# Attention kernel with two branches and a mixture of experts: scores for the maxima of two heads in one pair of wide matmuls

## The chip, the cores and the metric

The kernel runs on one core of one Trainium2 chip. The metric is the device time of one launch in microseconds, the median of several runs. Shares and stretches of the trace are of one profiled execution, whose own time stands beside the median below.

## What is computed

The input is 8 batches of 256 tokens of width 256. Each batch is normalised and goes through two attention branches of 16 heads, a latent one with rotary parts ("MLA") and a plain one with heads of 16 numbers ("MHA"); behind the plain one comes a mixture of 8 experts, top 2 per token. In the reference, cut to what matters here:

```python
xn = _layernorm(x)
s = _L0_attn_ref(xn, ...)                      # MLA, 16 heads, causal softmax
# plain branch (MHA), then the experts
q = (xn1 @ Wq.T).reshape(b, s, 16, 16); k, v likewise
attn = jnp.einsum('bqhd,bkhd->bhqk', q, k) * scale
attn = softmax(where(causal, attn, -inf))
h = jnp.einsum('bhqk,bkhd->bqhd', attn, v).reshape(b, s, hid)
x2 = residual + h @ Wo.T
out = x + s * silu(x2 + moe(rmsnorm(x2)))
```

The change touches the scores of the plain branch alone.

## The kernel before, in words

Every engine runs its own instruction list in program order, and semaphores tie the lists together. A batch b goes through four stages on TensorE (PE):

- **P2(b)**, `stage_p2`: the queries and keys of the plain branch, stacked 64 rows high per head (high part, low part, a row for the maximum), are transposed. There are 8 units u = 0 to 7, four transposes of 128x128 each, queries for even u and keys for odd u, into PSUM banks 3, 2, 0 in turn (`bank2`). ScalarE (ACT) copies each unit out, and VectorE (DVE) copies the lower 64 partitions of the units that hold queries (`odd_heads`). Between u = 0 and u = 1 PE also runs `to_tokens` of the batch before; DVE then makes `normalise` of it, behind its third `odd_heads`, and PE's `back` of it, first thing after the first head of T1, waits for that.
- **T1(b)**, `stage_t1`: for each of the 16 heads h, PE makes the transposed scores of the MLA branch (`scores1`, four FP32 matmul instructions), then `max2(b)` for head h - 1: the untransposed scores of the plain branch, from which DVE takes each query's maximum (`maxima`, a 128-column and a 256-column reduction per head). ACT exponentiates, GpSimd (POOL) masks, and `values(g)` multiplies by the values after heads 7, 11, 15 and after the stage. Other work is hung between heads by number: on PE `back` (0), `project` (3), `transpose_x` (10), `route_transpose` (11), `route_logits` (14); on DVE, in `stage_m2`, the residual `kept` (4), `stats_x2` (5), `copy_batch` (7), `copy_rms1` (8), `scale_x2` (9), `x_low` (12), and `top_two` behind the stage.
- **P1(b + 1)**, `stage_p1`: projections of the next batch in 18 steps. `values(3)` and the transposes of the maxima (`max_t`) come after step 0; step 1 waits for `ohd`, the end of DVE's `top_two`.
- **T2(b)**, `stage_t2`: transposed scores of the plain branch (`scores2`) with the maxima of the next batch's MLA branch between them (`max1`). It starts when the row of maxima, sent by `row2` through the DMA queue, has landed.

The last batch has no P1. After it come the experts.

In `max2`, head h uses bank 2 + h % 2 of PSUM (`ps[2]`, `ps[3]`), and its matmuls wait until DVE has done head h - 2 (`mx2`). A matmul here is 128 stationary columns (queries) against 128 or 256 moving columns (keys). The two heads of a pair lie in the upper and the lower 64 partitions: `kt2` holds both, `qt2` holds each head by itself with zeros in the other half, cleared once at the start.

Of the kernel before, what the change touches and what calls it, by code (L numbers as in the profile page):

```python
# [23 lines left out]
F32 = mybir.dt.float32  # L24
# [7 lines left out]
P = 128  # L32
# [58 lines left out]
def build(nc, x, w_cols, w_dq, w_uqr, w_dkv, w_ukv, w_out, w_o, w_ln1, w_ln2, w_r, w_experts,  # L91
          cosines, sines, ident, mask, upper, route_c, slots, out):
    ctx = ExitStack()
    with ctx:
# [80 lines left out]
        wo2 = sb("wo2", [P, ET, E], F32, late)  # L175
        qt2 = sb("qt2", [P, H, S], F32R, late)
        kt2 = sb("kt2", [P, H // 2, S], F32R, late)
        v2 = sb("v2", [P, 2, H, PADV], F32, late)
# [97 lines left out]
        t2e = sem("mha_qk_kept")  # L276
        t2o = sem("mha_q_odd_kept")
        m2d = sem("mha_scores")
# [83 lines left out]
        def _(sp):  # L362
# [21 lines left out]
            def row2(b):  # L384
                sp.wait_ge(mte2, b + 1)
                for e in range(2):
                    r = ST * e + MROW2
                    sp.dma_start(qt2[r:r + 1, e:H:2, :].bitcast(F32),
                                 mt[e * H // 2:(e + 1) * H // 2, :]).then_inc(md2, 16)
# [78 lines left out]
        def _(pool):  # L468
# [14 lines left out]
            nc.gpsimd.memset(ks[:, :, :, MROW2:MROW2 + 1].bitcast(F32), 1.0)  # L483
            nc.gpsimd.memset(qt2[:, :, :].bitcast(F32), 0.0).then_inc(clear, 1)

# [98 lines left out]
        def _(pe):  # L584
# [115 lines left out]
            def stage_p2(b, after):  # L700

                max_t(b, negm1, mx1, mtr1)
                for u in range(8):
# [4 lines left out]
                    if u >= 3:  # L708

                        wait(pe, t2e, 8 * b + u - 2)  # L710
                        if (u - 3) % 2 == 0:
                            wait(pe, t2o, 4 * b + (u - 3) // 2 + 1)
# [25 lines left out]
            def max2(b):  # L738
                def head(h):
                    if h == 0:  # L740
                        wait(pe, t2e, 8 * b + 8)
                        wait(pe, t2o, 4 * b + 4)
                    if h >= 2:
                        wait(pe, mx2, 16 * b + h - 1)
                    raw_scores(ps[2 + h % 2], qt2[:, h, :], kt2[:, h // 2, :]).then_inc(m2d, 1)
                return head
# [37 lines left out]
            def scores2(h, o):  # L784
                mm(o[:, 0:2 * P], kt2[:, h // 2, P:S], qt2[:, h, :], True, True)
                return mm(o[:, 2 * P:4 * P], kt2[:, h // 2, 0:P], qt2[:, h, :], True, True)

# [181 lines left out]
        def _(act):  # L969
# [100 lines left out]
            def stage_p2(b, after):  # L1070
                max_t1(b)
                wait(act, st2, 16 * b)
                for u in range(8):
                    wait(act, tr2, 8 * b + u + 1)
                    t = slice(u // 4 * P, (u // 4 + 1) * P)
                    a = bank2(u)[:, :].rearrange("p (h t) -> p h t", h=4)
                    if u % 2 == 0:

                        h0 = 8 * (u // 2 % 2)
                        copy(qt2[0:ST, h0:h0 + 8:2, t], a[0:ST, :, :]).then_inc(t2e, 1)  # L1080
                    else:
                        copy(kt2[:, 4 * (u // 2 % 2):4 * (u // 2 % 2) + 4, t], a).then_inc(t2e, 1)
                    after.get(u, lambda: None)()
# [151 lines left out]
        def _(dve):  # L1235
# [152 lines left out]
            def stage_m2(b, after):  # L1388
                wait(dve, mtr2, b)
                for h in range(H):  # L1390
                    maxima(b, h, (h % 2) * (H // 2) + h // 2, negm2, m2d, mx2)
                    after.get(h, lambda: None)()

# [26 lines left out]
            def odd_heads(b, i):  # L1420

                wait(dve, tr2, 8 * b + 2 * i + 1)
                t = slice(i // 2 * P, (i // 2 + 1) * P)
                h0 = 8 * (i % 2)
                copy(qt2[ST:P, h0 + 1:h0 + 8:2, t],
                     bank2(2 * i)[ST:P, :].rearrange("p (h t) -> p h t", h=4)).then_inc(t2o, 1)

# [320 lines left out]
```

## Time and profile before

| | us |
|---|---|
| median of 3 runs | 956.92 |
| lowest, highest | 955.44, 962.53 |
| profiled execution | 958.59 |
| its span, first to last instruction | 956.9 |
| mean granted TensorE clock | 0.935 of full |

The page gives busy time by engine, the span in slices, the DMA queues, the chain of work that ended last, and groups of instructions by line. `L586` is the helper that issues every matmul, so matmuls are told apart by their tiles and widths. Buffer numbers are left out of the names: `qt` stands for `qt` and `qt2`, `kt` for `kt` and `kt2`. "ps<-kt,qt" are the products of `max2` (keys moving), "ps<-qt,kt" those of `scores1` and `scores2`.

### The profile page before, as it was taken

The numbers are of one execution on the slowest core, as the hardware profiler recorded it, in microseconds if no ns is written. First come the engines' busy times: TensorE is split into PE (matmuls) and PEld (weight loads), VectorE is DVE, ScalarE is ACT, GpSimd is POOL, SyncE is SP. The second block draws the span as 40 slices with busy tenths as digits, with TensorE's granted clock in tenths as the row PEclk, the third lists the DMA queues.
The fourth block names the chain that finished last, engine by engine and source line by source line (L and its number), as shares of the span: only waits on it lengthen the run. The fifth ranks groups of instructions, "written<-read, shape, count | busy, mean of one in ns | idle before, by whom it ended". The sixth has DMA issues, their size and how long they took to land.

```text
span 956.9 us, 18123 instructions
## 1 busy us (share of the span) xinstructions
PE 830.5 (87%) x6432; PEld 743.6 (78%) x6432; DVE 625.2 (65%) x2207; ACT 501.6 (52%) x1089; POOL 392.2 (41%) x538
## 2 busy tenths in 40 slices
PE   5889999999999999999998998965269999998980
PEld 3868978978887887887897897843169999998980
DVE  4876677667677667757758757632257777776754
ACT  3445375366366456456356446540146677776651
POOL 5522432343343334344344344331404756555541
PEclk9878999999999999999999999976579999999995
DMA  8000000000000000000000000030236776889736
GB/s 273 1 1 2 13 1 25 12 2 13 24 1 14 13 13 2 24 12 3 23 13 2 24 12 3 23 144 23 47 134 176 221 220 198 238 240 348 193 53 186
DMA packets 39884, 71.04 MB, mean 74 GB/s; under 512 B 10914, under 2 KB 34850, under 8 KB 36834
## 3 DMA queue, kind: packets, MB, share of 16 engines
q1 hardware_dynamic: 29074, 57.39, 17.6%
q0 software_dynamic: 9856, 12.13, 6.7%
q8 instruction: 52, 0.85, 0.4%
q10 hardware_dynamic: 864, 0.36, 0.2%
q14 instruction: 38, 0.31, 0.1%
HBM read 55.12 MB, written 14.81 MB: 73 GB/s over the span
## 4 chain that ended last, share of the span: by engine, by line
PE 67%; DVE 10%; DMA 9%; issue 6%; POOL 2%; ACT 2%; SPq 2%; POOLq 0%; DVEq 0%; ACTq 0%
PE ps L586 54%; DMA expert_rows<-yo,slot_of 6%; PE ps L679 6%; PE ps L716 3%; DVE ps L1400 2%; PE ps L612 2%; DVE ps L1397 1%; SPq L425 1%; PE ps L621 1%; DVE qr L1237 1%; DMA w_ukv_raw<-in_w_ukv 1%; DMA raw<-in_w_experts 1%; SPq L441 1%; POOL slots L515 1%; POOL expert_rows L563 1%
## 5 line engine op out<-in xcount | busy, mean ns | idle before, releaser
L523 POOL TENSOR_SCALAR_AFFINE_SELECT ex<-ex 128x256 f32<-128x256 f32 x256 | 107.6, 425 | 246.5 <-ACT ex L1101 245.1
L1101 ACT ACTIVATE ex<-ps 128x384 f32<-128x384 f32 x256 | 125.4, 497 | 118.9 <-PE ps L586 116.8
L586 PE MATMUL ps<-qt,kt 128*128 128x256 f32 (+1 forms) x768 | 164.1, 325 | 8.6 <-ACT ex L1101 4.6
L502 POOL TENSOR_TENSOR tok<-tok,swp 128x256 f32<-128x256 f32 x128 | 97.4, 761 | 114.7 <-DVE swp L1362 113.7
L1397 DVE CUSTOM_DVE_ANT_0 ps<-ps,mask 128x128 f32<-128x128 f32 x256 | 77.4, 302 | 94.9 <-PE ps L586 90.5
L586 PEld LDWEIGHTS ps<-qt,kt 128*128 128x128 f32 x768 | 108.9, 193 | 20.7 <-issue 9.8
L563 POOL DMA_INDIRECT expert_rows<-yo,slot_of x46 | 78.5, 1707 | 110.8 <-DMA expert_rows<-yo,slot_of 55.6
L1400 DVE CUSTOM_DVE_ANT_0 ps<-ps,mask 128x256 f32<-128x256 f32 x256 | 118.9, 465 | 0.0
L1241 DVE TENSOR_TENSOR wel<-raw,weh 128x768 fp32r<-128x768 f32 x92 | 88.4, 961 | 37.2 <-ACT weh L971 36.0
L586 PE MATMUL ps<-wh,xth 128*128 128x320 f32 (+2 forms) x352 | 96.9, 358 | 3.7 <-DVE wl L1241 2.8
L1358 DVE TENSOR_TENSOR tok<-ps,cos_t 128x320 f32<-128x320 f32 x128 | 62.9, 491 | 52.8 <-PE ps L586 52.2
L586 PE MATMUL ps<-xeh,weh 128*128 128x256 f32 x368 | 79.4, 298 | 11.8 <-issue 9.9
L971 ACT ACTIVATE qt<-ps 128x512 f32<-128x512 f32 (+1 forms) x96 | 57.2, 596 | 61.9 <-PE ps L679 59.8
L971 ACT ACTIVATE kt<-ps 128x512 f32<-128x512 f32 (+1 forms) x96 | 57.4, 598 | 53.4 <-PE ps L679 48.3
L586 PE MATMUL ps<-wh,xtl 128*128 128x320 f32 (+2 forms) x352 | 84.1, 321 | 0.0
L586 PE MATMUL ps<-wl,xth 128*128 128x320 f32 (+2 forms) x352 | 83.8, 320 | 0.0
L971 ACT ACTIVATE weh<-raw 128x768 fp32r<-128x768 f32 x92 | 77.9, 846 | 10.1 <-DMA raw<-in_w_experts 10.1
L679 PE MATMUL ps<-idf,tok 128*128 128x128 f32 x512 | 77.0, 273 | 0.0
L586 PE MATMUL ps<-xeh,wel 128*128 128x256 f32 x368 | 75.9, 289 | 0.0
L586 PE MATMUL ps<-xel,weh 128*128 128x256 f32 x368 | 75.8, 288 | 0.0
L586 PE MATMUL ps<-kt,qt 128*128 128x128 f32 (+1 forms) x256 | 73.4, 368 | 0.0
L586 PE MATMUL ps<-kr,qr 128*128 128x128 f32 (+1 forms) x256 | 58.6, 316 | 16.8 <-DVE negm L1400 13.1
(160 smaller groups left out, 1918.3 us busy)
## 6 DMA issues: line engine op xcount, KB each, us to landing
raw<-in_w_experts SPq DMA_DIRECT2D x23, 1536.0 KB
mla_branch<-s_b SPq DMA_DIRECT2D x8, 256.0 KB, 2.1
expert_rows<-xn SPq DMA_DIRECT2D x8, 256.0 KB, 2.2
x_normalised<-otk SPq DMA_DIRECT2D x8, 256.0 KB, 2.1
xr<-in_x SPq DMA_DIRECT2D x1, 2048.0 KB
s_tok<-mla_branch SPq DMA_DIRECT2D x1, 2048.0 KB
w_cols_raw<-in_w_cols SPq DMA_DIRECT2D x1, 1792.0 KB, 15.4
x<-expert_rows SPq DMA_DIRECT2D x3, 512.0 KB, 5.2
```

The source lines that it names most:

```text
L502: nc.gpsimd.tensor_tensor(t, t, swp[:, n % 2, :, :], ALU.add).then_inc(tokd, 1)
L523: nc.gpsimd.affine_select(a, a, [[0, 2], [1, P]], ALU.is_ge, zero, 0, -1).then_inc(exm, 1)
L563: nc.gpsimd.indirect_dma_start(ys[:, :], bass.IndirectOffsetOnAxis(mt_b[:, blk, j, 1:2], 0), yo[:, blk % 2, j, :], None, compute_op=ALU.ad ...
L586: return nc.tensor.matmul(o, a, m, start=start, stop=stop, skip_group_check=True, **k)
L679: t = nc.tensor.transpose(ps[2 + n % 2][:, j * P:(j + 1) * P], tok[:, n % 4, j, :], idf[:, :])
L716: i = nc.tensor.transpose(bank2(u)[:, j * P:(j + 1) * P], a[:, p0:p0 + P], idf[:, :])
L971: return nc.scalar.activation(o, a, ACT.Copy)
L1101: nc.scalar.activation(ex[:, h % (2 * G), :], ps[4 + h % 2][:, P:4 * P], ACT.Exp, scale=scale).then_inc(ex_, 1)
L1241: return nc.vector.tensor_tensor(o, a, b.bitcast(F32), ALU.subtract)
L1358: nc.vector.tensor_tensor(tok[:, n % 4, :, 0:HW], a, cos_t[:, tt:tt + 1, :].broadcast_to([P, G, HW]), ALU.mult)
L1397: nc.vector.tensor_tensor_reduce(out=o[:, 0:P], in0=o[:, 0:P], in1=mask2[:, 1, :], scale=-1.0, scalar=-2.0 * BIG, op0=ALU.add, op1=ALU.min ...
L1400: nc.vector.tensor_tensor_reduce(out=o[:, S:2 * S], in0=o[:, S:2 * S], in1=mask2[:, :, :].rearrange("p a k -> p (a k)"), scale=-1.0, scala ...
```

## The change

The plain branch's queries are now kept in pairs (`qt2` has 8 columns of heads, both heads of a pair in it) and the keys per head with zeros in the other half (`kt2` has 16). One matmul with a pair's queries stationary and both heads' keys moving gives the scores of both heads: 256 columns for the first 128 queries (into `ps[3]`), 512 for the other 128 (into `ps[2]`). `max2` does nothing after even heads and issues both matmuls of a pair after the odd one; the first waits for DVE to have done the 128-wide reductions of the pair before, the second for its 256-wide ones. DVE reduces in the order first queries of both heads, other queries of both heads; its hung work keeps its numbers, counted now in half pairs. `odd_heads` now copies halves of the key units (odd u), so that each waits one unit longer. `scores2` reads pairs and heads the other way round, with the same sizes.

```diff
             def row2(b):
                 for e in range(2):
                     r = ST * e + MROW2
-                    sp.dma_start(qt2[r:r + 1, e:H:2, :].bitcast(F32),
+                    sp.dma_start(qt2[r:r + 1, :, :].bitcast(F32),
...
                         wait(pe, t2e, 8 * b + u - 2)
-                        if (u - 3) % 2 == 0:
+                        if (u - 3) % 2 == 1:
                             wait(pe, t2o, 4 * b + (u - 3) // 2 + 1)
...
             def max2(b):
                 def head(h):
-                    if h == 0:
+                    if h % 2 == 0:
+                        return
+                    j = h // 2
+                    if j == 0:
                         wait(pe, t2e, 8 * b + 8)
                         wait(pe, t2o, 4 * b + 4)
-                    if h >= 2:
-                        wait(pe, mx2, 16 * b + h - 1)
-                    raw_scores(ps[2 + h % 2], qt2[:, h, :], kt2[:, h // 2, :]).then_inc(m2d, 1)
+                    else:
+                        wait(pe, mx2, 16 * b + 2 * j - 1)
+                    mm(ps[3][:, 0:2 * P].rearrange("p (e k) -> p e k", e=2), qt2[:, j, 0:P],
+                       kt2[:, 2 * j:2 * j + 2, 0:P], True, True).then_inc(m2d, 1)
+                    if j > 0:
+                        wait(pe, mx2, 16 * b + 2 * j)
+                    mm(ps[2][:, :].rearrange("p (e k) -> p e k", e=2), qt2[:, j, P:S],
+                       kt2[:, 2 * j:2 * j + 2, :], True, True).then_inc(m2d, 1)
...
             def scores2(h, o):
-                mm(o[:, 0:2 * P], kt2[:, h // 2, P:S], qt2[:, h, :], True, True)
-                return mm(o[:, 2 * P:4 * P], kt2[:, h // 2, 0:P], qt2[:, h, :], True, True)
+                mm(o[:, 0:2 * P], kt2[:, h, P:S], qt2[:, h // 2, :], True, True)
+                return mm(o[:, 2 * P:4 * P], kt2[:, h, 0:P], qt2[:, h // 2, :], True, True)
...
                     if u % 2 == 0:
+                        copy(qt2[:, 4 * (u // 2 % 2):4 * (u // 2 % 2) + 4, t], a).then_inc(t2e, 1)
+                    else:
                         h0 = 8 * (u // 2 % 2)
-                        copy(qt2[0:ST, h0:h0 + 8:2, t], a[0:ST, :, :]).then_inc(t2e, 1)
-                    else:
-                        copy(kt2[:, 4 * (u // 2 % 2):4 * (u // 2 % 2) + 4, t], a).then_inc(t2e, 1)
+                        copy(kt2[0:ST, h0:h0 + 8:2, t], a[0:ST, :, :]).then_inc(t2e, 1)
...
             def stage_m2(b, after):
                 wait(dve, mtr2, b)
-                for h in range(H):
-                    maxima(b, h, (h % 2) * (H // 2) + h // 2, negm2, m2d, mx2)
-                    after.get(h, lambda: None)()
+                for j in range(H // 2):
+                    for t in range(2):
+                        wait(dve, m2d, 16 * b + 2 * j + t + 1)
+                        n = (t + 1) * P
+                        for e in range(2):
+                            o = ps[3 - t][:, e * n:(e + 1) * n]
+                            col = e * (H // 2) + j
+                            i = nc.vector.tensor_tensor_reduce(
+                                out=o, in0=o, in1=mask2[:, 1 - t:2, :].rearrange("p a k -> p (a k)"), scale=-1.0,
+                                scalar=-2.0 * BIG, op0=ALU.add, op1=ALU.min, accum_out=negm2[:, t, col:col + 1])
+                        i.then_inc(mx2, 1)
+                        after.get(2 * j + t, lambda: None)()
...
             def odd_heads(b, i):
-                wait(dve, tr2, 8 * b + 2 * i + 1)
+                wait(dve, tr2, 8 * b + 2 * i + 2)
                 t = slice(i // 2 * P, (i // 2 + 1) * P)
                 h0 = 8 * (i % 2)
-                copy(qt2[ST:P, h0 + 1:h0 + 8:2, t],
-                     bank2(2 * i)[ST:P, :].rearrange("p (h t) -> p h t", h=4)).then_inc(t2o, 1)
+                copy(kt2[ST:P, h0 + 1:h0 + 8:2, t],
+                     bank2(2 * i + 1)[ST:P, :].rearrange("p (h t) -> p h t", h=4)).then_inc(t2o, 1)
```

The clearing at the start moves from `qt2` to `kt2`, which now has the larger of the two sizes.

## Rows read from the trace of the kernel before

**Rows 1.** The page: busy us (share of the span) and instructions of each engine.

```profile
PE 830.5 (87%) x6432; PEld 743.6 (78%) x6432; DVE 625.2 (65%) x2207; ACT 501.6 (52%) x1089; POOL 392.2 (41%) x538
```

**Rows 2.** Busy time by stretch: us, busy us (instructions) per engine, clock, DMA share, GB/s.

```profile
219.86:294.39 74.53, 71.31 (x584) 62.54 (x582) 51.82 (x224) 40.16 (x87) 30.05 (x53) 1.00 0.04 13
294.39:370.44 76.05, 72.85 (x584) 64.05 (x583) 51.83 (x224) 40.16 (x87) 30.06 (x53) 0.98 0.04 12
...
298.99:322.82 23.83, 23.46 (x198) 19.69 (x196) 16.99 (x90) 12.04 (x28) 7.25 (x17) 1.00 0.07 24
```

**Rows 3.** Timeline, PE in T1(3): start us, us, instruction, count [idle before, releaser].

```profile
305.37 0.82 PE L586 MATMUL ps<-qt,kt 128*128 128x128 f32 x4
306.03 0.19 PEld L586 LDWEIGHTS ps<-kt,qt 128*128 128x128 f32 x1
306.14 0.31 PEld L586 LDWEIGHTS ps<-qt,kt 128*128 128x128 f32 x2
306.26 0.27 PE L586 MATMUL ps<-qt,kt 128*128 128x128 f32 x1
```

**Rows 4.** Timeline, PE in P1: matmuls of 512 moving columns.

```profile
347.65 0.63 PE L586 MATMUL ps<-wl,xth 128*128 128x512 f32 x2
348.12 0.63 PE L586 MATMUL ps<-wh,xtl 128*128 128x512 f32 x2
```

**Rows 5.** Timeline, DVE in T1(3): head 4, `kept`, head 6, `copy_batch`.

```profile
306.46 0.30 DVE L1397 CUSTOM_DVE_ANT_0 ps<-ps,mask 128x128 f32<-128x128 f32 x1
...
306.68 0.47 DVE L1400 CUSTOM_DVE_ANT_0 ps<-ps,mask 128x256 f32<-128x256 f32 x1
...
307.06 0.69 DVE L1342 TENSOR_TENSOR xn<-ps,xn 128x512 f32<-128x512 f32 x1
...
309.58 0.29 DVE L1397 CUSTOM_DVE_ANT_0 ps<-ps,mask 128x128 f32<-128x128 f32 x1
...
310.81 0.71 DVE L1237 COPY xb<-xn 128x512 f32<-128x512 f32 x1
```

**Rows 6.** Timeline, PE and DVE at the end of P2(3): units 4 and 5, `odd_heads`, `normalise`, `back`.

```profile
297.01 0.64 PE L716 MATMUL ps<-idf,qs 128*128 128x128 f32 x4
297.61 0.63 PE L716 MATMUL ps<-idf,ks 128*128 128x128 f32 x4
297.68 0.69 DVE L1237 CAST qt<-ps 64x512 fp32r<-64x512 f32 x1 [0.21 <-PE ps L716]
...
298.41 0.37 DVE L1322 RECIPROCAL rec<-ps 128x16 f32<-128x16 f32 x2
...
298.81 0.76 DVE L1327 TENSOR_TENSOR otk<-ps,rec 128x256 f32<-128x256 f32 x2
...
299.62 0.42 PEld L621 LDWEIGHTS ps<-idf,otk 128*128 128x128 f32 x4 [0.21 <-DVE otk L1327]
```

**Rows 7.** Timeline, PE and DVE, second half of T1(3) and start of P1(4).

```profile
311.66 0.30 PE L645 MATMUL ps<-idf,xb 128*128 128x128 f32 x1
...
317.44 1.06 PE L586 MATMUL ps<-wr,s_b 128*128 128x8 f32 x8 [0.23 <-ACT s_b L971]
...
320.20 0.50 PE L586 MATMUL ps<-kt,qt 128*128 128x128 f32 x2
...
320.74 0.30 DVE L1397 CUSTOM_DVE_ANT_0 ps<-ps,mask 128x128 f32<-128x128 f32 x1 [0.47 <-PE ps L586]
...
321.33 0.17 DVE L1502 MAX8 mx<-ps 128x8 f32<-128x8 f32 x1
...
322.60 0.17 DVE L1516 TENSOR_TENSOR ohb<-oh 128x16 bf16<-128x16 f32 x1
...
322.82 0.56 PE L586 MATMUL ps<-wh,xth 128*128 128x320 f32 x2
```

**Rows 8.** PE after a wait in T2: timeline, then busy time by stretch (columns of group 2).

```profile
354.26 0.77 PE L586 MATMUL ps<-kr,qr 128*128 128x128 f32 x2 [1.11 <-DVE negm L1400]
...
354.15:357.56 3.41, 3.30 (x15) 3.33 (x16) 2.35 (x15) 0.00 (x0) 0.29 (x1) 0.50 0.03 5
```

More of the change, by code:

```diff
@@ L175, in build @@
         wo2 = sb("wo2", [P, ET, E], F32, late)
-        qt2 = sb("qt2", [P, H, S], F32R, late)
-        kt2 = sb("kt2", [P, H // 2, S], F32R, late)
+        qt2 = sb("qt2", [P, H // 2, S], F32R, late)
+        kt2 = sb("kt2", [P, H, S], F32R, late)
         v2 = sb("v2", [P, 2, H, PADV], F32, late)
@@ L276, in build @@
         t2e = sem("mha_qk_kept")
-        t2o = sem("mha_q_odd_kept")
+        t2o = sem("mha_k_odd_kept")
         m2d = sem("mha_scores")
@@ L483, in _ @@
             nc.gpsimd.memset(ks[:, :, :, MROW2:MROW2 + 1].bitcast(F32), 1.0)
-            nc.gpsimd.memset(qt2[:, :, :].bitcast(F32), 0.0).then_inc(clear, 1)
+            nc.gpsimd.memset(kt2[:, :, :].bitcast(F32), 0.0).then_inc(clear, 1)
             def power(k, t):
```

## The prediction

> **What bounds the kernel now.** I read the page first: PE is the busiest engine, 87% of the span [rows 1]. Then busy time by stretch: a middle batch takes 74.5 us, or 76.0 when the granted clock falls to half once inside it [rows 2]; six of the eight batches have this shape. In T1, the stage that the change is about, PE is busy 23.46 of 23.83 us [rows 2]: it is the bound, and DVE, busy 16.99, is the next to be looked at. Last I read the timeline of T1 of the third batch (starting at 294.39), on which all times below stand. The reader should see three things in it: what a head costs PE, how early DVE delivers what PE waits for, and the three places where PE already meets DVE or ACT.
>
> **What PE saves.** One head of `max2` costs PE 0.23 us: its second load of queries starts at 306.03, the next load at 306.14, and the next head's scores at 306.26 [rows 3]. So the 128-column product holds the array for 0.11, as long as the next load takes, and the 256-column one for 0.12. Two heads cost 0.46. After the change a pair has one product of 256 columns, 0.12, and one of 512, whose price is read where the same type (FP32R) is used at that width: two of them take 348.12 - 347.65 = 0.47, so 0.235 each [rows 4]. The loads hide under the products before them (0.11 under 0.12, under 0.235 and under the last product of `scores1`). Pair: 0.35. Gain: 0.11 per pair, 8 pairs, 8 batches: 64 x 0.11 = 6.9 us if nothing else moves. The keys of a pair are read as two runs of 128 or one of 512 columns; no row shows what two runs cost. Bounds: nothing below, and above the rate of the FP32 products of `scores1`, 0.66 us for 768 columns [rows 3], or 0.66 for the pair, which would lose 0.2 per pair, 13 us. I take 0.35, since type and length are those of the nearest row.
>
> The Trainium skill (TensorE: Matmul & The Clock Gate, Back-to-back issue gap) gives about 131 ns per product of 512 columns in a stream of loads and products. By that figure, as an estimate, the second product would cost 0.10 less and the gain would be some 6.6 us larger; the trace's own 0.235 does not agree, and the sum goes by the trace.
>
> **What it costs at the front of T1.** The third `odd_heads` now waits for unit 5 instead of unit 4. Unit 4 starts at 297.01, unit 5 at 297.61, and DVE starts the copy 0.67 after unit 4 began [rows 6]. So the copy moves by 0.60. Right behind it on DVE are the reciprocals (298.41) and the products of `normalise` (298.81 + 0.76), and PE's `back` is already waiting for them, 0.21 idle [rows 6]. Nothing covers this: `back` goes from 299.62 to 300.22, and all of T1 behind it with it. +0.60 in the seven batches that have `normalise`. Unit 4 now waits for DVE's copy of half of unit 1, 0.69 long [rows 6], beside ACT's: a tenth at most, left out. The fourth `odd_heads` has over a microsecond before the first pair needs it. What ACT copies in P2 has the same sizes in another order, and `scores2`, the clearing and `row2` keep their sizes: nothing.
>
> **What it costs in the middle.** DVE's work per head is 0.60 (306.46 to 307.06) [rows 5], 1.20 per pair. Before, a head's matmuls waited for the head two before them, 1.78 earlier, which DVE had done after 1.06, so 0.7 was to spare; now the second product of a pair waits for the whole pair before. DVE starts 306.46 - 306.14 = 0.32 after the 256-column product gets the array [rows 3, 5], and is done 0.32 + 1.20 + 0.14 = 1.66 after it. The next pair comes 2 x 0.66 + 0.35 = 1.66 later, its second product at 1.78. It just fits, with nothing to spare for DVE's hung work. From head 4 on this work is dense. Heads 4 to 7 with `kept` and `stats_x2` run without a break from 306.46 to 310.81, 4.35 us [rows 5], and then comes `copy_batch`, 0.71, for which `transpose_x` waits.
>
> After the change DVE can start heads 4 and 5 only when pair 2 is there. Before, the product of head 5 reached the array at 306.26 + 0.66 = 306.92. Now: + 0.60 (front) - 0.22 (two pairs saved) - 0.23 (head 4 is no longer ahead of it) = 307.07. DVE starts at 307.39 and reaches `copy_batch` 4.35 later, at 311.74. The same point is the end of pair 3, so pair 4's second product cannot start before about 311.74 + 0.14 + 0.1 = 311.98. `transpose_x`, right behind it, stood at 311.66 [rows 7] and would be due at 311.66 + 0.60 - 5 x 0.11 = 311.71, so the product was due 0.235 earlier, at 311.48: a stall of 0.5. `transpose_x` then waits for the copy until 311.74 + 0.71 = 312.45 and starts near 312.53 instead of 311.66. So the whole loss at this point is +0.87, and it already contains the 0.60 of the front and the gain of five pairs. `values(0)` also waits for `kept`, some 0.4, which the same stall absorbs. Pair 5 gives back 0.11: +0.76.
>
> **What it costs at the end.** The routing products, which wait for ACT, not PE (0.23 idle at 317.44 [rows 7]), shift by that 0.76; what PE gains just before them is lost in their wait. Head 14's product, 0.23, is gone from behind them. The last pair therefore comes at 320.20 + 0.76 - 0.23 = 320.73. Before, DVE began the last head 0.54 after its first load and worked 0.59, to 321.33 [rows 7]. Now it begins 0.11 + 0.32 = 0.43 after the load, and has two heads, 1.20: 322.36. `top_two` is 322.60 + 0.17 - 321.33 = 1.44 long, and step 1 of P1 starts 0.05 after it, at 322.82 [rows 7]. After: 322.36 + 1.44 + 0.05 = 323.85. **+1.0 us per middle batch.** From there PE's order and loads are as before.
>
> **The sum.** Batches 1 to 6 (counted from 0): 6 x 1.03 = +6.2. Batch 0 has no `normalise`, no hung work of the routing and no `top_two`: the whole gain, -0.9. The last batch has no `copy_batch`: front +0.60, six pairs -0.65, the stall +0.5, head 14 -0.23, the longer tail of DVE (1.63 instead of 1.13) +0.5: +0.6 to +0.7. Together +5.9 us on the profiled execution's 958.59 (956.9 span and 1.7 around it), or +0.6%. That execution is 1.7 above the median; on the median, 956.92 + 5.9 = 962.8 us.
>
> **The clock.** After 1.11 us of idle at 354.26 the granted clock is 0.50 for 3.41 us, the lower of its two levels, 1.2 GHz [rows 8]; a batch with such a drop takes 76.05 instead of 74.53, 1.5 us more [rows 2]. Three of the six middle batches have one; others have a wait as long without it. The new stalls, 0.8 at `back`, 0.4 and 0.5 around pair 4, 0.7 before step 1, are shorter, so I take no new drops; but shifts decide which waits cost one, and 1.5 us more or less per batch is open.
>
> **Rivals.**
> - *PE's saving alone counts.* DVE's lateness is hidden: `normalise` was not the last thing that `back` needed, and the hung work fits in between. Then -6.9 us: 950.0. For it: PE is 98% busy in T1. Against: `back` waits for DVE already [rows 6]. It decides if unit 5 ends no later than DVE could use it. Faster, but within 1%. 0.10.
> - *Only one of the two costs is real.* Without the front's 0.60 the middle stall grows as DVE is then the bound from pair 2 on, but all shifts by 0.60 less: +5.9 - 7 x 0.6 = +1.7, 958.6. Without the longer tail of DVE (0.5 each): +5.9 - 3.5 = +2.4, 959.3. Together 0.20.
> - *The stalls pull the clock down.* The stall at pair 4 and the wait for the copy lie within 1.2 us of each other. If they cost one drop in each of the seven batches: +5.9 + 7 x 1.5 = +16.4, 973.3; in three or four of them, 968. For it: 0.8 us idle there against 1.11 where a drop was seen. Against: products lie between. 0.18.
> - *The wide product is slow* on keys in two runs, up to 0.66 for a pair: past the point where a pair costs 0.46 PE loses in every batch, up to +13 more. 0.03.
> - *The wide product is quick*, less than half of [rows 4]: some 6.6 more gained than in the first rival, 943. Nothing in the trace speaks for it: 0.01. That is what the page of the Trainium skill named above would give.
> - My forecast, 962.8, its own range 960 to 966: 0.48.
>
> **Chances and range.** Within 1% is about what a measurement of this kernel can tell from no change: 947.3 to 966.5. Slower by over 1% are most of the clock rival, the slow product, and the upper edge of mine with a drop or two: 0.22. Faster by over 1% needs the quick product or the first rival with fewer drops: 0.03. The rest, 0.75, lies within. The range reaches from near the first rival to the middle of the clock rival: 952 to 970.
>
> **What would show it.** In the trace of the changed kernel: products of `max2` 0.12 and 0.235 apart; `back` waiting 0.8 for DVE where it waited 0.21; a wait of PE for `negm` before the fifth pair and for `xb` before `transpose_x`; step 1 of P1 about 29.4 us after the batch's first transpose instead of 28.4; batches of 75.5 us, or 77 with a clock drop. It is wrong if `back` keeps its place, if T1 shows no wait for `negm`, or if batches are shorter than 74.5.

## The result and the profile after

| | kernel before | kernel after |
|---|---|---|
| median | 956.18 us | 968.49 us |
| lowest to highest of 4 runs each | 954.51 to 962.53 | 966.96 to 974.06 |
| profiled execution | 958.59 us | 969.09 us |
| its span | 956.9 us | 967.4 us |
| middle batch without, with a clock drop | 74.5, 76.0 us | 76.0, 77.5 us |

The ratio is 1.0127, with a 95% interval of 1.0065 to 1.0189: slower by 1.3%. The same kernel measured again beside the experiments gave 968.32 us and a ratio of 1.0092 [1.0056, 1.0129]. So the loss is certain and its size is about 1%. The forecast was 962.8, with a range of 952 to 970: the sign was right, the size about half of what came. (The medians differ by 12.3 us here and by 8.8 in the repetition, the profiled spans by 10.5; the accounts below go by the spans.) One of the 32 runs of the kernel before beside the later experiments (1195 us) and one of the 12 of `e6_all` (1355 us) were slow, at a granted clock of 0.64 and 0.55; the ratios leave them out.

The page of the kernel after, busy us and instructions of each engine:

```profile
PE 827.1 (85%) x6304; PEld 727.4 (75%) x6304; DVE 624.8 (65%) x2207; ACT 501.5 (52%) x1089; POOL 391.2 (40%) x538
```

Against [rows 1] PE has 128 matmuls fewer and is busy 3.4 us less, while the span is 10.5 us longer. DVE and ACT have the same work as before. So what was lost is waiting, not work, and it has to be looked for in idle time. Busy time by stretch (us, busy us and instructions of PE, PE's loads, DVE, ACT, POOL; clock, DMA share, GB/s), batches 2 and 3:

```profile
220.92:298.47 77.55, 72.68 (x567) 62.09 (x566) 52.07 (x224) 40.28 (x87) 29.81 (x53) 0.98 0.04 12
298.47:374.49 76.02, 71.08 (x568) 60.79 (x567) 51.96 (x224) 40.18 (x87) 29.79 (x53) 1.00 0.04 12
```

Beside [rows 2], batches without a drop: 76.02 us instead of 74.53, with PE busy 71.08 instead of 71.31. PE's idle time went from 3.2 to 4.9 us per batch. What PE waited for in batches 1 to 6 (releaser: us in total, times, longest us):

```profile
PE ps L586 <- DVE negm L1417: 10.5, 12, 1.5
PE ps L586 <- DVE ohb L1533: 3.2, 6, 0.6
...
PE ps L621 <- DVE otk L1335: 2.5, 6, 0.4
PE ps L586 <- DVE xn L1350: 2.3, 6, 0.4
```

Once in each batch: 0.53 for the rows that `top_two` writes (`ohb`) ahead of step 1, 0.41 at `back` (`otk`), 0.39 at `values(0)` for `kept` (`xn`). The first line is a wait in T2, in another part of the batch; the same line of the kernel before is

```profile
PE ps L586 <- DVE negm L1400: 8.9, 12, 1.5
```

It grew by 1.6 us, and the forecast had nothing there.

**T1 of the same batch as in [rows 3] to [rows 7].** It starts at 298.47 here and at 294.39 there, so a time of before has its place 4.08 later. PE:

```profile
304.37 0.66 PE L621 MATMUL ps<-idf,otk 128*128 128x128 f32 x4 [0.41 <-DVE otk L1335]
...
312.83 0.86 PE L586 MATMUL ps<-ex,v 128*32 128x256 f32 x16 [0.39 <-DVE xn L1350]
...
315.85 0.78 PE L586 MATMUL ps<-kt,qt 128*128 128x256 f32 x2
316.73 0.63 PE L645 MATMUL ps<-idf,xb 128*128 128x128 f32 x4
...
322.40 1.06 PE L586 MATMUL ps<-wr,s_b 128*128 128x8 f32 x8 [0.28 <-ACT s_b L979]
...
328.07 0.56 PE L586 MATMUL ps<-wh,xth 128*128 128x320 f32 x2 [0.53 <-DVE ohb L1533]
```

DVE:

```profile
303.15 0.37 DVE L1330 RECIPROCAL rec<-ps 128x16 f32<-128x16 f32 x2
...
315.93 0.66 DVE L1245 COPY xb<-xn 128x512 f32<-128x512 f32 x1
...
325.36 0.30 DVE L1405 CUSTOM_DVE_ANT_0 ps<-ps,mask 128x128 f32<-128x128 f32 x1 [1.56 <-PE ps L586]
...
326.59 0.17 DVE L1519 MAX8 mx<-ps 128x8 f32<-128x8 f32 x1
...
327.84 0.17 DVE L1533 TENSOR_TENSOR ohb<-oh 128x16 bf16<-128x16 f32 x1
```

Measured from the batch's start, the points that the forecast named, in us (the profiled executions; the same in all six middle batches to a few hundredths):

| point | before | after | shift | forecast |
|---|---|---|---|---|
| `back` [rows 6] | 5.25 | 5.90 | +0.65 | +0.60 |
| `transpose_x` [rows 7] | 17.27 | 18.26 | +0.99 | +0.87 |
| routing products [rows 7] | 23.05 | 23.93 | +0.88 | +0.76 |
| step 1 of P1 [rows 7] | 28.43 | 29.60 | +1.17 | +1.03 |

The transposes of the maxima, which follow the last pair and on which the experiments are also read, went from 27.90 to 28.68. The chain of the forecast is there link by link. The reciprocals begin 0.66 later and `back` idles 0.41. `copy_batch` (315.93) ends at 316.59, and `transpose_x`, which stands behind it, starts at 316.73. The last pair's reductions run from 325.36 to the MAX8 of `top_two` at 326.59, 1.23 for two heads where [rows 7] has 0.59 for one, and step 1 starts 0.06 after `ohb` is done.

Two of the signs that the forecast named have to be looked at closely. `back` idles 0.41 on PE; the 0.8 of the forecast is the wait of its loads, 0.81 here, which stood at 0.21 before. And T1 shows no wait of PE for `negm`, which the forecast had called a sign that it is wrong. All that is left of this wait is small: the load of the second product of a pair that follows right on another waits 0.10 (at 311.29, for DVE's end of the pair before), and costs PE 0.06.

### The profile page after: what moved, and what is told of

Read it like the earlier page. It is cut to its first block, busy times and chain, and to the rows that moved or that the text cites. A ratio compares the mean times of both kernels' runs of the same rounds, so it can differ in the third digit from the quotient of the medians.

```text
span 967.4 us, 17859 instructions
## 1 busy us (share of the span) xinstructions
PE 827.1 (85%) x6304; PEld 727.4 (75%) x6304; DVE 624.8 (65%) x2207; ACT 501.5 (52%) x1089; POOL 391.2 (40%) x538
## 4 chain that ended last, share of the span: by engine, by line
PE 53%; DMA 14%; DVE 14%; issue 11%; POOL 4%; ACT 2%; SPq 1%; POOLq 0%; DVEq 0%; ACTq 0%
PE ps L586 41%; DMA expert_rows<-yo,slot_of 11%; PE ps L679 5%; PE ps L716 3%; DVE ps L1417 2%; PE ps L612 2%; POOL expert_rows L563 1%; DVE ps L1405 1%; DVE ps L1414 1%; DMA ln<-in_w_ln 1%; POOL xg L552 1%; PE ps L621 1%; DVE qr L1245 1%; POOL slots L515 1%; DVE otk L1335 1%
## 5 line engine op out<-in xcount | busy, mean ns | idle before, releaser
L586 PE MATMUL ps<-qt,kt 128*128 128x256 f32 (+1 forms) x768 | 160.6, 328 | 8.4 <-ACT ex L1109 4.4
L586 PEld LDWEIGHTS ps<-qt,kt 128*128 128x128 f32 x768 | 115.0, 195 | 24.8 <-ACT ex L1109 9.9
L1405 DVE CUSTOM_DVE_ANT_0 ps<-ps,mask 128x128 f32<-128x128 f32 (+1 forms) x256 | 85.0, 385 | 57.1 <-PE ps L586 56.9
L1196 ACT ACTIVATE sg<-ps 128x256 f32<-128x256 f32 x92 | 35.7, 388 | 70.5 <-PE ps L586 67.8
L586 PEld LDWEIGHTS ps<-xeh,weh 128*128 128x128 f32 x368 | 58.2, 196 | 15.8 <-issue 15.8
```

The lines of the kernel that those rows point to most:

```text
L586: return nc.tensor.matmul(o, a, m, start=start, stop=stop, skip_group_check=True, **k)
L1196: nc.scalar.activation(sg[:, n % 2, :], ps[n % 3][:, 0:BS], ACT.Silu).then_inc(sgd, 1)
L1405: i = nc.vector.tensor_tensor_reduce(out=o, in0=o, in1=mask2[:, 1 - t:2, :].rearrange("p a k -> p (a k)"), scale=-1.0, scalar=-2.0 * BIG, ...
```

## The experiments

Nine kernels were made of the two, each run beside the kernel before; the kernel after was run once more with them. What is read from each is the place of a point after its batch's start, in the profile, and the median of its runs.

| kernel | `back` | `transpose_x` | maxima transposes | step 1 | PE's wait in T2 | batch, no drop | ratio to before |
|---|---|---|---|---|---|---|---|
| before | 5.25 | 17.27 | 27.90 | 28.43 | 1.11 or 1.48 | 74.5 | 1 |
| after | 5.90 | 18.26 | 28.68 | 29.60 | 1.48 | 76.02 | 1.0127 |
| `e8_after_again` | 5.90 | 18.27 | 28.68 | 29.61 | 1.48 | 76.03 | 1.0092 |
| `e1_layout` | 5.90 | 17.94 | 28.56 | 29.09 | 1.48 | 75.55 | 1.0055 |
| `e2_norm_first` | 5.32 | 17.63 | 28.05 | 28.98 | 1.48 | 75.41 | 1.0031 |
| `e3_top_early` | 5.90 | 18.27 | 28.68 | 28.82 | 1.11 or 1.49 | 74.88 | 1.0061 |
| `e4_base_late` | 5.90 | 18.27 | 28.68 | 29.61 | 1.10 | 75.66 | 1.0058 |
| `e5_copy_early` | 5.90 | 18.00 | 28.47 | 29.40 | 1.49, once 1.11 | 75.87 | 1.0081 |
| `e6_all` | 5.32 | 17.37 | 27.84 | 27.98 | 1.11 | 74.05 | 0.9963 |
| `e7_before_moves` | 5.25 | 17.28 | 27.87 | 28.02 | 1.10 | 74.04 | 0.9942 |
| `e9_pairs_clean` | 5.32 | 16.91 | 26.85 | 27.00 | 1.10 | 73.02 | 0.9899 |
| `e10_heads_clean` | 5.25 | 17.27 | 27.37 | 27.51 | 1.10 | 73.73 | 0.9965 |

The 73.73 of `e10_heads_clean` is of batch 1, its only one without a drop. Batch 1 is about 0.2 longer than the later ones in other kernels too (76.22 and 76.03 in `e8_after_again`), so its later batches would be near 73.5.

### The new layout with products per head (`e1_layout`)

Queries stay in pairs and keys padded, `odd_heads` and its waits are those of after; only the products go by head, and DVE reduces head by head as in the kernel before.

```diff
-                    mm(ps[3][:, 0:2 * P]..., qt2[:, j, 0:P], kt2[:, 2 * j:2 * j + 2, 0:P], True, True)
...
-                    mm(ps[2][:, :]..., qt2[:, j, P:S], kt2[:, 2 * j:2 * j + 2, :], True, True)
+                    raw_scores(ps[2 + h % 2], qt2[:, h // 2, :], kt2[:, h, :]).then_inc(m2d, 1)
```

> The new layout (queries in pairs, keys padded) and the later odd_heads, but max2 and stage_m2 head by head as before: 128 and 256 columns per head. Theory (the later copy delays normalise and back by 0.6, and the rest of the loss is the pairing): back 5.9 us after the batch's first transpose (before 5.25, after 5.90), step 1 of P1 at 28.4 + 0.6 = 29.0 (before 28.4, after 29.6), median 956.2 + 7 x 0.6 = 960.5; if the wait for DVE in T2 stays at 1.48 instead of 1.12, 2 more. Rival (the front costs nothing in the end, the pairs alone do): step 1 at 28.4, 956 to 957. Other rival (the padded keys themselves are slower in scores2 or max2): over 966 with longer products.

Measured: `back` +0.65, step 1 at 29.09, 964.31 us (10 runs; before beside it 959.29), ratio 1.0055 [1.0033, 1.0077]. Of e1's timeline, `back` and step 1 of P1, the batch from 297.24:

```profile
303.14 0.44 PE L621 MATMUL ps<-idf,otk 128*128 128x128 f32 x2 [0.42 <-DVE otk L1327]
...
326.33 0.56 PE L586 MATMUL ps<-wh,xth 128*128 128x320 f32 x2
```

The shift is the same at `back` (0.65) and at step 1 (29.09 - 28.43 = 0.66): the layout alone costs the front and nothing behind it. From here to the kernel after, the wide products make step 1 another 0.51 later, where their saving on PE should have made it earlier. The loss in T1 thus has two parts of about equal size, one of the layout, one of the wide products.

### `normalise` ahead of the third copy of the odd heads (`e2_norm_first`)

```diff
                 odd_heads(b, 1)
+                normalise()
                 odd_heads(b, 2)
-                normalise()
                 odd_heads(b, 3)
```

> The changed kernel with normalise ahead of the third odd_heads on DVE. Theory: back no longer waits for DVE, 5.05 instead of 5.90 after the first transpose, and since DVE's dense stretch is tied to pair 2, which comes earlier with it, step 1 of P1 moves by the same 0.85 to 28.75; seven batches: 968.5 - 6 = 962.5. Rival (T1 is bound by DVE or ACT further on, which start no earlier): back early but step 1 still at 29.3 or later, 966 to 968.5.

Measured: `back` at 5.32, step 1 at 28.98, 962.72 us (10 runs), ratio 1.0031 [1.0003, 1.006]. `back` and step 1 in e2's timeline, the batch from 293.92:

```profile
299.24 0.60 PE L621 MATMUL ps<-idf,otk 128*128 128x128 f32 x4
...
322.90 0.56 PE L586 MATMUL ps<-wh,xth 128*128 128x320 f32 x2 [0.53 <-DVE ohb L1533]
```

The wait at `back` is gone and T1 ends 0.62 earlier, all of what `back` gained (0.58), and no more: the front was a pure shift, and the end's wait of 0.53 is untouched by it. `back` did not come to the expected 5.05: it now stands right behind the first head's scores, as in the kernel before, and these start 0.06 later than there (4.66 after the batch's start instead of 4.60). That is what the layout costs in P2 apart from `normalise`: unit 4 starts at 2.86 instead of 2.62, and most of it is caught up by unit 7.

### `top_two` ahead of the last pair (`e3_top_early`)

```diff
+                if not first:
+                    after[13] = lambda: top_two(b - 1)
                 stage_m2(b, after)
-                if not first:
-                    top_two(b - 1)
```

> The changed kernel with top_two moved ahead of the last pair's reductions, into DVE's idle 1.6 us. Theory (step 1 waits for DVE's longer tail, two heads instead of one, plus top_two): step 1 comes right behind the transposes of the maxima, 28.95 instead of 29.6; six batches: 968.5 - 4 = 964.5. Rival (the tail is not what step 1 waits for, or the reductions of the last pair are pushed back by top_two and the transposes with them): 29.4 to 29.6, 967 to 969.

Measured: maxima transposes unchanged at 28.68, step 1 at 28.82, 964.36 us (10 runs), ratio 1.0061 [1.0038, 1.0084]. e3's timeline, the batch from 293.09:

```profile
321.77 0.39 PE L602 MATMUL ps<-idf,negm 128*16 128x128 f32 x2
321.91 0.54 PE L586 MATMUL ps<-wh,xth 128*128 128x320 f32 x2
```

Step 1 follows the transposes by 0.14 with no wait, where it was 0.92 in the kernel after. So 0.78 of T1's end was `top_two` standing behind the tail of DVE. In the kernel before the same distance was 0.53: part of this wait was there all along.

### The update of `base` behind the casts (`e4_base_late`)

This is the step in T2 that the forecast did not have. In `positions`, DVE adds the counts to `base` ahead of the casts to `meta`; here it does so after them, and the counts that DVE and PE wait for are moved with it.

```diff
                 dve.wait_ge(pst, 6 * r + 2)
-                nc.vector.tensor_tensor(base[:, :], ps[1][:, 2 * NE:3 * NE], base[:, :], ALU.add)...
...
                 i.then_inc(pst, 1)
+                nc.vector.tensor_tensor(base[:, :], ps[1][:, 2 * NE:3 * NE], base[:, :], ALU.add)...
```

> The changed kernel with the update of base in positions moved behind the two casts to meta, so that these casts reach DVE 0.08 to 0.2 us earlier against POOL's select. Theory (in T2 the second cast is held up for 0.24 us when POOL's select has started 34 to 41 ns after the first cast, and not when it starts 44 to 46 ns after it): the wait of PE in T2 falls from 1.48 to 1.1 in all six middle batches, 968.5 - 2.2 = 966.3, and fewer clock drops. Rival (the longer wait in T2 comes of something else that the change moved, POOL only happens to be there): the wait stays at 1.48 or moves by 0.1, 968 to 969.

Measured: T1 unchanged (29.61), PE's wait in T2 1.10 in all six middle batches, a batch 75.66 instead of 76.02, 964.92 us (10 runs), ratio 1.0058 [1.0034, 1.0082]. The result is the expected one, but the casts came earlier by far less than the 0.08 to 0.2 expected: 2.393 to 2.396 us after the product of the ranks instead of 2.400 to 2.407, some 0.01. That this was enough is described in the last section.

### `copy_batch` by the second head (`e5_copy_early`)

```diff
-                    after[7] = lambda: copy_batch(b + 1)
+                    after[1] = lambda: copy_batch(b + 1)
```

> The changed kernel with copy_batch hung behind the first pair (number 1) instead of number 7, where DVE is idle for 1.8 us. Theory (transpose_x waits for the copy, and DVE's dense stretch before it holds up the fifth pair): transpose_x goes from 18.26 after the batch's first transpose to 17.9, step 1 from 29.6 to 29.25; six batches: 2 us less than the changed kernel. The 0.4 that values(0) waits for kept stays. Rival (ScalarE's routing copy is what the rest of T1 waits for, so the gain is lost there): step 1 at 29.5 or later, no change.

Measured: `transpose_x` at 18.00, step 1 at 29.40, 965.67 us (10 runs; before 959.49), ratio 1.0081 [1.0054, 1.0107]. In e5's timeline, the batch from 299.57, the wait for `kept` is still there:

```profile
313.94 0.86 PE L586 MATMUL ps<-ex,v 128*32 128x256 f32 x16 [0.38 <-DVE xn L1350]
...
317.57 0.60 PE L645 MATMUL ps<-idf,xb 128*128 128x128 f32 x4
```

Taking the copy away from `transpose_x` gains 0.26 there and 0.20 at step 1, less than the 0.35 expected. Of the waits, the one for `kept` is left in the middle; `e9_pairs_clean` below moves it, together with `stats_x2`.

### All four moves on the pairs (`e6_all`) and on the kernel before (`e7_before_moves`)

`e6_all` is the kernel after with the edits of e2, e3, e4 and e5. `e7_before_moves` is the kernel before with those of e3, e4 and e5 (in its order `normalise` has no later copy ahead of it).

> The changed kernel with all four moves: normalise first, top_two early, base late, copy_batch early. Theory (each wait is its own, and they add): step 1 at 29.6 - 0.6 - 0.8 - 0.35 = 27.9, wait in T2 at 1.1, a middle batch without a clock drop 74.0 instead of 76.0, and 0.5 shorter than the kernel before: 0.995 of it. Rival (the moves hide behind each other, since one bound lies beneath all of them): step 1 at 28.3 to 28.8 and no faster than the kernel before.

> The kernel before with the moves that it allows: top_two early, base late, copy_batch early (normalise has to stay behind the third odd_heads there, as the bank of unit 4 is needed for unit 7). Tells whether the pairs are worth anything once the waits are gone. Theory: step 1 28.43 - 0.3 = 28.1, wait in T2 at 1.1 in all batches, middle batch 74.2: 0.997 of the kernel before, 0.2 us per batch more than with pairs. Rival (the pairs save their 0.11 each once nothing waits): e6_all ahead by 0.9 us per batch, 0.6%.

Measured: `e6_all` 955.57 us (12 runs), ratio 0.9963 [0.9941, 0.9984]; `e7_before_moves` 954.04 (12 runs), ratio 0.9942 [0.9918, 0.9967]; both beside 959.49 of before. Busy time by stretch of an undropped batch, e6:

```profile
215.80:289.85 74.05, 70.52 (x567) 60.97 (x566) 51.55 (x224) 40.08 (x87) 30.10 (x53) 1.00 0.04 13
```

and e7:

```profile
217.51:291.55 74.04, 71.02 (x583) 62.49 (x582) 52.01 (x224) 40.11 (x87) 29.92 (x53) 1.00 0.04 13
```

Three things follow. The waits of T1 add: step 1 gains 0.62 (e2) + 0.78 (e3) + 0.20 (e5) = 1.60 one by one, and 29.60 - 27.98 = 1.62 together. With these waits out of the way the pairs are a little faster than the kernel before. But the kernel before gains the same from the same moves: 74.04 and 74.05 for a batch, where PE is busy 0.5 less with the pairs. The pairs' saving is still lost in a wait. e6's timeline, the batch from 289.85, shows two:

```profile
303.59 0.86 PE L586 MATMUL ps<-ex,v 128*32 128x256 f32 x16 [0.37 <-DVE xn L1350]
...
312.94 1.06 PE L586 MATMUL ps<-wr,s_b 128*128 128x8 f32 x8 [0.27 <-ACT s_b L979]
```

### The waits for `kept` and for ACT out of the way (`e9_pairs_clean`, `e10_heads_clean`)

On `e6_all`, DVE's `kept` moves behind the first pair, `stats_x2` behind the second, and on ACT `keep_yt` one head earlier. `e10_heads_clean` is `e7_before_moves` with `keep_yt` moved alone; it has no wait for `kept`.

```diff
-                    after[13] = lambda: keep_yt(b - 1)
+                    after[12] = lambda: keep_yt(b - 1)
...
-                    after[1] = lambda: copy_batch(b + 1)
+                    after[1] = lambda: (copy_batch(b + 1), kept())
```

> e6_all with the last three waits of PE in T1 taken away: kept and copy_batch behind the first pair, stats_x2 behind the second, ScalarE's routing copy keep_yt one head earlier. In e6_all PE still waited 0.37 us for kept before values(0), 0.3 for scale_x2 and 0.4 for keep_yt. Theory (the pairs do save about 0.1 each, and each of these waits gave it back): transposes of the maxima at 27.1 to 27.3 after the batch's first transpose instead of 27.84, middle batch 73.5 instead of 74.05, 0.992 to 0.993 of the kernel before. Rival (in T1 ScalarE's exponentials and DVE's reductions of the pair before set the pace, so the pairs cannot save): 27.6 or later, 0.995 or more.

> e7_before_moves, head by head, with keep_yt one head earlier as well: the same moves on the kernel before. Theory: transposes of the maxima at 27.5 instead of 27.87, middle batch 73.7, 0.992 to 0.993 of the kernel before; e9_pairs_clean then 0.2 to 0.3 us per batch ahead, 0.1 to 0.2% of the whole. Rival (the pairs cannot save): e10_heads_clean as fast or ahead.

Measured: `e9_pairs_clean` 950.07 us (6 runs; before 958.99), ratio 0.9899 [0.9873, 0.9925]; `e10_heads_clean` 955.28 us (11 runs), ratio 0.9965 [0.9949, 0.998]. e9, the batch from 292.48, routing products without a wait and the maxima transposes:

```profile
314.68 0.95 PE L586 MATMUL ps<-wr,s_b 128*128 128x8 f32 x8
...
319.31 0.39 PE L602 MATMUL ps<-idf,negm 128*16 128x128 f32 x2
```

e10, the batch from 216.76, the same transposes:

```profile
244.13 0.39 PE L602 MATMUL ps<-idf,negm 128*16 128x128 f32 x2
```

The maxima transposes stand at 26.85 and 27.37, and the pairs are further ahead than the 0.2 to 0.3 expected. With no wait of PE shown in T1 of either, the eight pairs save 0.52 us per batch, 0.065 each. (The two kernels also differ in the layout, 0.07 at `back` against the pairs, and in the place of `normalise`, `kept` and `stats_x2`.) `e9_pairs_clean` is the fastest kernel of the study, 1.0% below the kernel before and 1.9% below the kernel after (950.07 against 968.32, both near a median of before of 959). Not all of the 5.2 us between e9's and e10's medians need be the pairs: of the 5.5 between their profiled spans, 6 x 0.52 = 3.1 are the pairs', and 3 are clock drops, of which e9 has three in the middle batches and e10 five, at 1.5 us each (the last batch and the experts took 0.6 more in e9).

### The kernel after once more (`e8_after_again`)

> The changed kernel as it is, beside the others on one chip, for its ratio from more runs. By the stretches of its trace, without clock drops and with the long wait in T2 in all six middle batches against two of six: 6 x 1.16 + 4 x 0.37 + 0.7 = 9.1 us, 1.009 to 1.010. If the drops also come more often with the longer wait, 1.012 or more.

Measured: 968.32 us (9 runs, before 959.49 in 32), ratio 1.0092 [1.0056, 1.0129]; every point of T1 within 0.01 of the first profile, T2's wait 1.48 in all six batches, three clock drops. The shares of T1 and T2 below are thus no accident of one execution. Those of the start and the end of the span are: here batch 0 ends at 141.49 and not at 143.19, and the last batch and the experts take 362.92 and not 361.78.

## Why the prediction was right, and where it was not

The two spans differ by 967.4 - 956.9 = 10.5 us. They split like this, against +5.9 forecast:

| part | forecast | measured | how |
|---|---|---|---|
| up to the end of batch 0 | -0.9 | -0.06 | 63.58 instead of 63.64 from the first scores on, which start at 79.61 in both |
| T1, batches 1 to 6 | +6.2 | +7.0 | 6 x 1.17 |
| T2's wait, batches 1 to 6 | 0 | +1.5 | 1.48 instead of 1.11 in four batches |
| clock drops, batches 1 to 6 | 0 | +1.5 | four instead of three |
| last batch and experts | +0.6 | +0.7 | 361.78 instead of 361.07 |
| sum | +5.9 | +10.6 | |

Two rows of this table owe something to luck. That the first scores start at 79.61 in both is chance (77.91 in `e8_after_again`). And the last row agrees by chance: at the end of T1 of the last batch the loss is twice the forecast, +1.39 (transposes of the maxima 28.06 after the batch's start instead of 26.67; 28.07 in `e8_after_again`), and what comes after it happened to be shorter. From that batch's start to the end of the program the twelve profiles lie between 357.86 and 365.12, and one kernel's two at 361.78 and 362.92. The forecast of this batch lacked two new waits of PE, 0.41 for `scale_x2` and 0.45 for the last maxima.

**The front** was right: forecast +0.60, measured +0.65, and e2, which moves `normalise` ahead of the later copy alone, gives back 0.58. The other 0.07 is the wait of unit 4, which the forecast had seen and left out. The rival that only one of the two costs is real falls with e2 and e3 together: each gives back its own share, 0.62 and 0.78.

**The middle** was right in size, +0.87 against +0.99, and in its cause, DVE's work between the pairs and `transpose_x`: DVE's stretch from the start of pair 2 (311.54) to `copy_batch` (315.93) took 4.39 where 4.35 was forecast. The order of PE's waits was another. The forecast put a stall of 0.5 before the second product of pair 4, with the wait for `kept` inside it. In the trace the wait for `kept` comes first (0.39 at 312.83), pair 4 then looks as in batch 0, where neither `kept` nor `stats_x2` hangs ahead of it (its two products take 0.78, and 0.77 there), and the rest is the wait for the copy, from the end of pair 4 to 316.73. e5 confirms the copy as the smaller part (0.20 of step 1). e9 against e6 moves `kept` and `stats_x2` (and `keep_yt`): `transpose_x` comes 0.46 earlier, 16.91 instead of 17.37, and `keep_yt` has no part in that (17.28 and 17.27 in e7 and e10).

**The end** was right in its mechanism, and e3 shows its whole price, 0.78. The forecast had +1.03 at this point and +1.17 was measured; 0.05 of the difference is the front; 0.07 more is already there at `transpose_x`; the last 0.02 is not traced.

**PE's saving** is the term that was mis-sized: 0.11 for every pair, 6.9 us in all. The price of a pair that waits for nothing was right. Two pairs with scores between them, in T1 of the batch from 298.47:

```profile
309.37 0.70 PE L586 MATMUL ps<-kt,qt 128*128 128x256 f32 x2
309.91 1.47 PE L586 MATMUL ps<-qt,kt 128*128 128x128 f32 x8
311.03 0.76 PE L586 MATMUL ps<-kt,qt 128*128 128x256 f32 x2
311.63 0.82 PE L586 MATMUL ps<-qt,kt 128*128 128x128 f32 x4
```

They are 1.66 apart, as forecast; the kernel before needs 1.77 (2 x 0.88). But the second of them keeps the next scores waiting for 0.60 instead of 0.54, since its second product waits for DVE, and so half of its saving is gone. Three pairs of a middle batch stand like this. In T1(0), which has neither `back`, `kept` nor `top_two` in it, hardly anything is saved. Three of the places that lose it can be seen. Scores that now follow directly on scores meet ACT's exponential, as at the loads

```profile
81.01 0.52 PEld L586 LDWEIGHTS ps<-qt,kt 128*128 128x128 f32 x4 [0.33 <-ACT ex L1109]
...
82.77 0.52 PEld L586 LDWEIGHTS ps<-qt,kt 128*128 128x128 f32 x4 [0.24 <-ACT ex L1109]
```

The first `values` is 0.19 ahead of before (86.36, 86.55), but only because head 6's products, 0.23, no longer stand ahead of it: the three pairs before it have saved nothing. `transpose_x`, which waits for the copy behind two heads of DVE here too, is 0.07 ahead (90.02, 90.09), with ten heads done in both. And `x_low` (`xtl`, 0.69 on DVE) now stands between the narrow and the wide reductions of a pair, so that the last pair's second product waits. PE and DVE after:

```profile
96.40 0.84 PE L586 MATMUL ps<-kt,qt 128*128 128x256 f32 x2
97.08 0.46 PE L586 MATMUL ps<-wh,xth 128*128 128x320 f32 x2
```

```profile
95.22 0.69 DVE L1249 TENSOR_TENSOR xtl<-ps,xth 128x512 fp32r<-128x512 f32 x1
95.83 0.42 DVE L1405 CUSTOM_DVE_ANT_0 ps<-ps,mask 128x256 f32<-128x256 f32 x1
96.17 0.14 DVE L1405 DVE_READ_ACCUMULATOR2_ANT negm<- 128x1 f32 x1
96.17 0.47 DVE L1405 CUSTOM_DVE_ANT_0 ps<-ps,mask 128x256 f32<-128x256 f32 x1
```

The last pair holds PE for 0.68, where the last head of before took 0.33 (96.81 to 97.14), the pair's saving and 0.1 more gone. At the end of T1(0) the maxima transposes of after and of before stand at

```profile
98.84 0.39 PE L602 MATMUL ps<-idf,negm 128*16 128x128 f32 x2
```

```profile
98.90 0.39 PE L602 MATMUL ps<-idf,negm 128*16 128x128 f32 x2
```

while the scores of both start at 79.61. The whole gain of eight pairs in batch 0 is 0.06 us instead of 0.9. The step that failed is "Batch 0 has no `normalise`, no hung work of the routing and no `top_two`: the whole gain": batch 0 does have `copy_batch` and `x_low`. The copy is the small part: with it moved (e5, e6, e9) these transposes come 19.17 after the scores' start instead of 19.23 (19.29 before). `x_low` and the wait for the exponential stayed where they are in every run; how much each of them takes was not tried. In the middle batches, with the waits out of the way in both forms (e9 against e10), the eight pairs save 0.52 and not 0.9; 0.18 of the rest is the three pairs that wait 0.06 for DVE. I had laid DVE's 1.20 per pair beside the pair's 1.66 and written "nothing to spare", and then followed this only around pair 4 and at the end.

**T2** was not in the forecast at all; "from there PE's order and loads are as before" took the stage for unchanged. Its instructions are, but the wait of PE there has two lengths, 1.11 and 1.48, and the kernel before already had both (four batches of one, two of the other). I had seen 1.11 in [rows 8] and not asked why batches 1 and 5 differed. 1.5 of the missing 4.6 us is this.

**The clock.** The new waits of PE in T1, 0.4 to 0.6, cost no drop in any profile: in all twelve, every drop inside the middle batches begins 58 to 63 us after the batch's start, between 0.3 before and 1.3 after the end of the wait in T2. So the rival that T1's stalls pull the clock down is not borne out. The number of drops in the six middle batches goes from one to five over the profiles, without following the kernel: e10 has five and e3 and e4 one, at waits of the same length. With 1.5 us each that is part of what single executions differ by (the kernel before alone spread from 953 to 965), and one drop more is another 1.5 us of the missing 4.6.

**The other rivals.** That the wide product is slow, or quicker than 0.235, is out: a free pair costs PE 0.34 (1.66 less 2 x 0.66 for the scores of two heads [rows 3]), the 0.35 taken, so keys in two runs cost nothing that can be read here. The page of the Trainium skill that the forecast named for 131 ns (TensorE: Matmul & The Clock Gate, Back-to-back issue gap) would, as an estimate, have made the free pair cost 0.25, and the trace does not agree here either. That PE's saving alone counts is not what happened; even in e9, with the waits moved away, the pairs' own share is 0.52 of 0.9 per batch.

## What to carry to other kernels

Wider products halve the number of points where an engine hands over, and each handover then stands for twice the work: before counting PE's saving, lay the receiving engine's whole work per wide step beside the producer's pitch, and look at what is queued behind the first and behind the last step. When a change makes an engine late, try the order of its side tasks before giving the change up: moves of lines that compute nothing new were worth more (three of them 1.62 us in T1 per batch, a fourth 0.37 in T2) than the change cost (1.17 and 0.37), and part of that helped the old form too: with its own moves it was as fast per batch as the pairs with theirs (74.04 and 74.05). Compare the two forms only after both have had the same moves.

## What the runs showed of the hardware

PE's wait for `negm` in T2 is 1.11 or 1.48 and nothing between, and it turns on a few nanoseconds between two other engines. Kernel before, batch 2, a short one (DVE, POOL and PE):

```profile
278.09 0.23 DVE L1237 CAST meta<-rc 128x4 uint32<-128x4 f32 x2
278.14 1.07 POOL L523 TENSOR_SCALAR_AFFINE_SELECT ex<-ex 128x256 f32<-128x256 f32 x2 [0.49 <-ACT ex L1101]
278.53 0.41 DVE L1237 CAST qr<-qt 128x512 fp32r<-128x512 f32 x1
279.74 0.47 PE L586 MATMUL ps<-kr,qr 128*128 128x128 f32 x2 [1.12 <-DVE negm L1400]
```

Kernel after, batch 3, a long one:

```profile
357.87 0.47 DVE L1245 CAST meta<-rc 128x4 uint32<-128x4 f32 x2
357.91 0.90 POOL L523 TENSOR_SCALAR_AFFINE_SELECT ex<-ex 128x256 f32<-128x256 f32 x2 [0.49 <-ACT ex L1109]
358.45 0.64 DVE L1245 CAST qr<-qt 128x512 fp32r<-128x512 f32 x1
359.88 0.47 PE L586 MATMUL ps<-kr,qr 128*128 128x128 f32 x2 [1.48 <-DVE negm L1417]
```

DVE casts twice in a row, 4 numbers per partition each, and POOL's affine select starts 34 to 50 ns after the first cast, ahead of the second. The pair of casts takes 0.23 or 0.47; the second alone 0.16 or 0.40. In the long case the next cast (`qr`) also starts 0.14 later (0.58 instead of 0.44 after the first cast) and takes 0.64 instead of 0.41: together the 0.37 by which PE's wait is longer. Over the 72 middle batches of the twelve profiles: where the select starts 43 ns or less after the first cast, the second cast is long; where it starts 45 ns or more after it, the cast is short, and POOL's select takes 0.45 instead of 0.41; 44 ns is seen with both. The kernel after has 34 to 41 (six long), before 42 to 46 (two long), e4 46 to 48 (none). In `e4_base_late` the select stands where it stands in the kernel after (0.906 to 0.908 us after the first instruction of `positions`, against 0.906 to 0.909), and the casts come some 10 ns earlier (0.859 or 0.860 against 0.865 to 0.874): the offset grew by that, and so its wait got shorter.

The Trainium skill (SBUF — State Buffer, Who interferes with whom) says that DVE and GpSimd share a port pair under an exclusive lock, and that when DVE works in a mode that takes both ports, which casts can, whichever issues first blocks the other for its whole instruction. By that rule, the trace agrees in that one of the two is held up in each case, never both; which of them issued first the trace does not tell, since cast, select and cast start in the same order in both cases. From the kernel before to the kernel after it is the select that comes earlier, 0.906 to 0.909 instead of 0.914 to 0.916, with the casts in place (0.865 to 0.874, and 0.869 to 0.874). Why the change moves it by these 8 ns stays open.
